# Projecting q and k already turned, and rotating them across partitions with block exchanges by DMA, in a fused attention and FFN kernel

## The chip, the cores and the metric

The kernel runs on one core of one Trainium2 chip. The metric is the device time of one execution in microseconds (us). The kernel before takes 277.16 us, the median of 3 runs (276.86 to 277.42). TensorE is called PE here, VectorE DVE, ScalarE ACT, GpSimd POOL and SyncE SP.

## The reference, cut to what matters

Inputs are x of 8 batches of 1024 tokens by 128, one head of width 128, and an FFN with hidden width 512. Everything is float32. The attention sees `i >= j` only.

```python
def fractional_rope(x, base):                      # first 64 of the 128 features turn, 64 do not
    rot, skip = jnp.split(x, 2, axis=-1)
    even, odd = jnp.split(rot, 2, axis=-1)         # 32 and 32
    return jnp.concatenate([even * cos - odd * sin, even * sin + odd * cos, skip], axis=-1)

q = fractional_rope(x @ wq) / sqrt(128);  k = fractional_rope(x @ wk) / sqrt(128);  v = x @ wv
p = softmax(q @ k.T - 1e30 * (i < j))
x = layernorm(x + (p @ v) @ wo)
h = gelu(x @ (alpha1 * sign(w1)).T + b1)           # exact gelu
x = layernorm(x + h @ (alpha2 * sign(w2)).T + b2)
```

## The kernel before

One batch c (0 to 7) at a time goes through a pipeline of stages, and neighbouring batches overlap. Every engine has a list of calls, written out by hand, which is its program: `scores(3, B - 4)` in PE's list is row tile 3 of batch 4 (B is 8). Engines meet in semaphores alone, and a call that waits holds up all that stands behind it on its engine. This also holds for SP, which issues nearly all DMAs.

A batch has 8 row tiles of 128 tokens, in two halves h. Products that need more than bfloat16 are made of fp32r parts: a value is split into a rounded part (`_hi`) and the rest (`_lo`), and three matmuls (hi by hi, hi by lo, lo by hi) replace one. The stages of a batch:

- SP loads x by stripes (`stripes`), DVE turns it in 32 by 32 squares (`x_squares`), ACT makes `xT_hi`, POOL `xT_lo`.
- `project(h, c)`: 4 token tiles times 3 matmuls of 256 columns each put q and k of half h, tokens on partitions, into a PSUM pair (two banks).
- `rotate(h, c)` on DVE: three products from PSUM with the tables; `rotation_sum` on POOL adds them into `tok`; `tok_copy` on ACT moves the 64 features that do not turn.
- `turn_qk(n, c)`, n from 0 to 3: 4 transposes of 128 by 128 on PE bring q or k of one half into a bank with the features on partitions; `qkT_high` (ACT) and `qkT_low` (DVE) write `qkT_hi` and `qkT_lo`.
- `scores(r, c)` on PE, `row_max` on DVE, `exponentials` on ACT, `turn_row` on DVE (32 by 32 squares); `carry(g, c)` on SP completes the transpose of the probabilities by 16 DMAs for rows 0 to 3 (g = 0), 16 for rows 4 to 7 (g = 1). `weigh_group(g, ..., c)` multiplies by x, `project_out` by wv times wo. Rows 4 to 7 of batches 0 and 7 are turned by PE instead.
- `residual1`, `statistics1` and `first_norm` (DVE), `first_factors` (POOL), `turn_x1`, `up`, `gelu`, `hidden_high` (ACT), `hidden_low` (POOL), `down`, `y_half`, `turn_y`, `residual2`, `statistics2`, `second_factors`, `second_norm` are the first norm, the FFN and the second norm; `store` writes the result.

Three PSUM pairs go round among projections, scores and `up`, and two banks among the rest (`next_pair`, `next_bank`). A call that takes a pair waits until the call three pairs ago has been read. `qkT_hi` and `qkT_lo` exist once: batch c overwrites batch c - 1 there.

Of the kernel before, what the change touches and what calls it, by code (L numbers as in the profile page):

```python
# [5 lines left out]
F32 = mybir.dt.float32  # L6
# [10 lines left out]
def attention_ffn_kernel(nc, x, wq, wk, wv, wo, w1, b1, w2, b2, cos_t, sin_t, out):  # L17
# [12 lines left out]
    P = 128  # L30
# [25 lines left out]
    with ctx:  # L56
# [10 lines left out]
        cos_sb = sb("cos_sb", [P, NT, ROT])  # L67
        sin_sb = sb("sin_sb", [P, NT, ROT])
# [17 lines left out]
        rot_cos = sb("rot_cos", [P, NG, TG, 2, ROT])  # L86
        rot_sin = sb("rot_sin", [P, NG, TG, 2, ROT])
        tok = sb("tok", [P, NT, QK])
# [34 lines left out]
        w2_sb = hid[:, 3, 0:H]  # L123
        w_raw = hid[:, 3, H:H + 2 * D]
# [9 lines left out]
        s_bias_in = sem("s_bias_in")  # L134
        s_xq_in = sem("s_xq_in")
# [68 lines left out]
        def _(sp):  # L204
# [15 lines left out]
            sp.dma_start(b2_sb[:, :], b2.rearrange("(p a) -> p a", a=1)).then_inc(s_bias_in, 16)  # L220

# [36 lines left out]
            stripes(2)  # L258
            carry(0, 0)
            stripes(3)  # L260
            tokens(1)
            stripes(B - 4)
            carry(0, 1)
            carry(1, 1)
            tokens(2)
            stripes(B - 3)
            carry(0, 2)
            carry(1, 2)
            stripes(B - 2)
            tokens(3)  # L270
            carry(0, 3)
            carry(1, 3)
            stripes(B - 1)
            carry(0, B - 4)
            tokens(B - 4)
            tokens(B - 3)
            carry(1, B - 4)
            carry(0, B - 3)
            tokens(B - 2)
            store(0)  # L280
            carry(1, B - 3)
            carry(0, B - 2)
            store(1)
            carry(1, B - 2)
            store(2)
            tokens(B - 1)
            carry(0, B - 1)
            store(3)
            store(B - 4)
            store(B - 3)  # L290
            store(B - 2)
            store_half(0, B - 1)
# [5 lines left out]
        def _(pool):  # L298
# [38 lines left out]
            def xT_low(h, c):  # L337
                pool.wait_ge(s_xT_hi[h], c + 1)
                if c > 0:
                    pool.wait_ge(s_qk[h], c)  # L340
# [3 lines left out]
            def rotation_sum(h, c):  # L344
                pool.wait_ge(s_rot_mul[h], c + 1)
                if c > 0:
                    pool.wait_ge(s_qkT[2 * h + 1], c)
                four = tok[:, TG * h:TG * (h + 1), :].rearrange("p n (j d) -> p n j d", d=D)
                pool.tensor_tensor(four[:, :, :, 0:ROT], rot_cos[:, h, :, :, :], rot_sin[:, h, :, :, :],  # L349
                                   ALU.add).then_inc(s_rot_add[h], 1)  # L350
# [45 lines left out]
            rotation_sum(0, 1)  # L396
            rotation_sum(1, 1)
            xT_low(0, 2)
            xT_low(1, 2)
            rotation_sum(0, 2)  # L400
# [3 lines left out]
            rotation_sum(1, 2)  # L404
            rotation_sum(0, 3)
            first_factors(1, 0)
            xT_low(0, B - 4)
            xT_low(1, B - 4)
            rotation_sum(1, 3)
            first_factors(0, 1)  # L410
            first_factors(1, 1)
            rotation_sum(0, B - 4)
            rotation_sum(1, B - 4)
            hidden_low(0, 0)
            hidden_low(1, 0)
            hidden_low(2, 0)
            xT_low(0, B - 3)
            hidden_low(3, 0)
            first_factors(0, 2)
            xT_low(1, B - 3)  # L420
            first_factors(1, 2)
            rotation_sum(0, B - 3)
            xT_low(0, B - 2)
# [3 lines left out]
            hidden_low(3, 1)  # L427
            first_factors(0, 3)
            second_factors(0)
            rotation_sum(1, B - 3)  # L430
            first_factors(1, 3)
            xT_low(1, B - 2)
            hidden_low(0, 2)
            rotation_sum(0, B - 2)
# [50 lines left out]
        def _(pe):  # L485
# [9 lines left out]
            def wait_freed(task, i, c):  # L495
# [7 lines left out]
                if task == "qk":  # L503
                    pe.wait_ge(s_tok[i], c + 1)
                if task == "up":
                    pe.wait_ge(s_gelu[i], c + 1)
# [1624 lines left out]
```

## Time and profile before

| | |
|---|---|
| time, median of 3 runs | 277.16 us |
| span of the profiled execution, first to last instruction | 274.5 us |
| median time less this span | 2.7 us |
| PE, DVE, ACT, POOL busy | 95%, 84%, 82%, 61% |
| matmul instructions | 1485 |
| bytes moved by DMA | 31.94 MB |

No time of the profiled execution beyond its span is listed; the 2.7 us are the median less the span and stand for what lies around it. The page lists busy time by engine, and the chain that ended last: PE holds 81% of it. SP's time isn't in the busy shares, since issuing a DMA isn't counted as work; it is seen in the timeline alone. Durations of neighbouring instructions on PE and DVE overlap, so that the distance between two starts is what one instruction takes from its engine.

### The profile page before, as it was taken

Reading aid. Unit: us, or ns where it says so; the run is one execution under the profiler, and the core shown is the slowest. Engines: PE = TensorE matmul, PEld = TensorE weight load, DVE = VectorE, ACT = ScalarE, POOL = GpSimd, SP = SyncE. Lnnn points to the kernel's source line nnn. Section 1 sums busy time; section 2 is a strip of 40 time slices with the busy share of each in tenths; the row PEclk is TensorE's granted clock in tenths of the full one; section 3 lists DMA queues with packets and bytes.
Section 4 is the critical chain, followed back from the end, with each engine's and each line's share of the span. In section 5 each row is a group of like instructions: output and inputs, shape, how many; then the busy total and the mean of one; then the engine's idle time right before and its main releaser. Section 6 shows DMA issues by size and latency. Waiting matters only on the chain.

```text
span 274.5 us, 5184 instructions
## 1 busy us (share of the span) xinstructions
PE 260.9 (95%) x1485; PEld 208.7 (76%) x1487; DVE 229.6 (84%) x638; ACT 224.7 (82%) x398; POOL 167.2 (61%) x258
## 2 busy tenths in 40 slices
PE   7899999999999999999999999999999999999960
PEld 3678989987779588868879688868886878897630
DVE  2799999999999996999979987998689738537984
ACT  3378964565897989996998999898999799999972
POOL 3033132613625698399821998497819887887772
PEclk9999999999999999999999999999999999999997
DMA  7944596479657936833685318825830720200323
GB/s 178 166 61 87 107 145 98 115 163 192 104 132 160 199 94 153 180 47 78 173 187 127 82 39 249 184 71 151 189 73 27 197 55 2 76 2 0 111 90 108
DMA packets 58012, 31.94 MB, mean 116 GB/s; under 512 B 33408, under 2 KB 54400, under 8 KB 57984
## 3 DMA queue, kind: packets, MB, share of 16 engines
q1 hardware_dynamic: 57024, 30.76, 50.4%
q10 hardware_dynamic: 960, 0.85, 1.3%
q8 instruction: 12, 0.20, 0.3%
q14 instruction: 16, 0.13, 0.2%
HBM read 9.18 MB, written 4.19 MB: 49 GB/s over the span
## 4 chain that ended last, share of the span: by engine, by line
PE 81%; DVE 6%; ACT 5%; issue 3%; DMA 2%; ACTq 1%; POOL 0%; POOLq 0%
PE pair L589 18%; PE bank L606 18%; PE bank L632 5%; PE bank L674 4%; PE pair L650 4%; PE pair L651 4%; PE bank L620 4%; PE bank L682 4%; PE bank L683 4%; PE bank L719 2%; DMA sin_sb<-in_sin_dram 2%; PE pair L663 2%; PE pair L665 2%; PE pair L664 2%; PE bank L639 2%
## 5 line engine op out<-in xcount | busy, mean ns | idle before, releaser
L391 POOL TENSOR_TENSOR hid_lo<-hid,hid_hi 128x1024 fp32r<-128x1024 f32 x28 | 66.0, 2386 | 19.7 <-ACT hid_hi L1075 19.7
L1004 ACT ACTIVATE prob<-pair,negmax 128x128 f32<-128x128 f32 (+3 forms) x64 | 47.2, 742 | 14.2 <-DVE negmax L1457 12.5
L606 PE MATMUL bank<-probT,xa 128*128 128x512 f32 (+3 forms) x160 | 54.2, 482 | 0.0
L1457 DVE CUSTOM_DVE_ANT_0 pair<-pair,mask_row 128x128 f32<-128x128 f32 (+3 forms) x64 | 47.9, 759 | 6.1 <-PE pair L589 5.5
L606 PEld LDWEIGHTS bank<-probT,xa 128*128 128x128 f32 x160 | 29.1, 190 | 20.2 <-issue 15.3
L341 POOL TENSOR_TENSOR xT_lo<-xT,xT_hi 128x512 fp32r<-128x512 f32 x14 | 18.0, 1288 | 40.4 <-ACT xT_hi L1034 40.4
L1467 DVE STREAM_TRANSPOSE turned<-prob 128x128 f32<-128x128 f32 (+7 forms) x56 | 39.5, 724 | 0.5 <-ACT prob L1004 0.5
L589 PE MATMUL pair<-qkT_hi 128*128 128x512 f32 (+3 forms) x96 | 36.0, 375 | 0.8 <-DVE qkT_lo L1619 0.3
L1068 ACT ACTIVATE hid<-pair,b_sb,alpha 128x1024 f32<-128x1024 f32 x28 | 32.9, 1209 | 0.1
L589 PE MATMUL pair<-qkT_lo,qkT_hi 128*128 128x512 f32 (+3 forms) x96 | 32.8, 342 | 0.0
L589 PE MATMUL pair<-qkT_hi,qkT_lo 128*128 128x512 f32 (+3 forms) x96 | 32.8, 342 | 0.0
L1075 ACT ACTIVATE hid_hi<-hid 128x1024 fp32r<-128x1024 f32 x28 | 28.6, 1057 | 0.0
L335 POOL TENSOR_TENSOR ln<-ln,minus_half 128x4 f32<-128x4 f32 (+1 forms) x21 | 26.2, 1249 | 1.6
L1102 ACT ACTIVATE res<-res,ln 128x128 f32<-128x128 f32 x52 | 23.1, 496 | 3.6 <-POOL ln L377 3.6
L1056 ACT ACTIVATE qkT_hi<-bank 128x512 fp32r<-128x512 f32 x32 | 18.5, 598 | 7.3 <-PE bank L674 7.2
L1619 DVE TENSOR_TENSOR qkT_lo<-bank,qkT_hi 128x512 fp32r<-128x512 f32 x32 | 21.1, 680 | 3.4 <-ACT qkT_hi L1056 3.4
L349 POOL TENSOR_TENSOR tok<-rot_cos,rot_sin 128x512 f32<-128x512 f32 x14 | 18.0, 1288 | 9.4 <-DVE rot_sin L1614 9.4
L650 PE MATMUL pair<-x1T_hi,sgn1T 128*128 128x512 f32 x56 | 23.4, 418 | 0.3 <-issue 0.3
L682 PE MATMUL bank<-hid_hi,sgn2T 128*128 128x512 f32 x56 | 22.3, 399 | 0.0
L683 PE MATMUL bank<-hid_lo,sgn2T 128*128 128x512 f32 x56 | 22.2, 396 | 0.0
L651 PE MATMUL pair<-x1T_lo,sgn1T 128*128 128x512 f32 x56 | 22.1, 395 | 0.0
L1567 DVE TENSOR_TENSOR res<-bank,x 128x512 f32<-128x512 f32 x16 | 10.9, 687 | 12.5 <-PE bank L719 12.4
(116 smaller groups left out, 649.9 us busy)
## 6 DMA issues: line engine op xcount, KB each, us to landing
probT<-turned SPq DMA_DIRECT2D x96, 116.0 KB, 2.3
probT<-turned SPq DMA_DIRECT2D x128, 52.0 KB, 2.0
xq<-in_L_attn_x_dram SPq DMA_DIRECT2D x28, 128.0 KB, 4.0
xa<-in_L_attn_x_dram SPq DMA_DIRECT2D x7, 512.0 KB, 4.7
out_dram<-res SPq DMA_DIRECT2D x7, 512.0 KB, 3.3
hid<-in_L_ffn_w_dram SPq DMA_DIRECT2D x2, 256.0 KB, 3.2
out_dram<-res SPq DMA_DIRECT2D x2, 256.0 KB, 2.3
xa<-in_L_attn_x_dram SPq DMA_DIRECT2D x1, 256.0 KB, 3.6
```

Source lines behind the costliest of these rows:

```text
L391: pool.tensor_tensor(hid_lo[:, j, :], hid[:, j, :], hid_hi[:, j, :].bitcast(F32), ALU.subtract).then_inc(s_hid_lo[j], 1)
L589: ins = pe.matmul(dst[:, lo:hi], qp[:, 0, me], kp[:, 1, lo - first:hi - first], start=n == 0, stop=n == 2)
L606: ins = pe.matmul(bank_of["px", g, c][:, 0:n * P], xa[c % 2][:, j, :], probT[g][:, :, TG * j:TG * j + n, :].rearrange("p n m i -> p m n i" ...
L650: pe.matmul(dst[:, half(h)], sgn1T[:, j, :], x1T_hi[:, half(h)], start=True, stop=False)
L651: ins = pe.matmul(dst[:, half(h)], sgn1T[:, j, :], x1T_lo[:, half(h)], start=False, stop=True)
L682: pe.matmul(dst[:, :], sgn2T[:, j, :], hid_hi[:, j, half(h)], start=j == 0, stop=False)
L683: ins = pe.matmul(dst[:, :], sgn2T[:, j, :], hid_lo[:, j, half(h)], start=False, stop=j == NF - 1)
L1004: act.activation(prob[r % 3][:, 0:(r + 1) * P], pair_of["score", r, c][:, slice(*columns(r))], ACT.Exp, scale=-1.0, bias=negmax[:, r:r + 1 ...
L1068: act.activation(hid[:, j, :], pair_of["up", j, c][:, :], ACT.Gelu, bias=b1_sb[:, j:j + 1], scale=alpha1[:, j:j + 1]).then_inc(s_gelu[j], 1)
L1075: act.activation(hid_hi[:, j, :], hid[:, j, :], ACT.Copy).then_inc(s_hid_hi[j], 1)
L1457: dve.tensor_tensor_reduce(mine, mine, mask_row[:, T - (r + 1) * P:T], -1.0, -MASKED, ALU.add, ALU.min, negmax[:, r:r + 1]).then_inc(s_max ...
L1467: dve.transpose(turned[g][:, :, squares(r, 0, r), :].rearrange("p k m j -> p m k j"), prob[r % 3][:, 0:(r + 1) * P].rearrange("p (m k j) - ...
```

## The change

Batch 0 is computed as before. From batch 1 on, q and k are projected with the weights as the stationary operand and x as the moving one, so the result has the features on partitions at once. The weight columns are reordered: `project_rot` gives the 64 turning features of q and the 64 of k, `project_skip` the 64 others of each; each is 6 matmuls of 512 columns. The rotation then needs the partner 32 features away, that is 32 partitions away. ACT copies the turning part into `rotT`, SP exchanges its four blocks of 32 partitions into `swapT` (`swap`, 4 DMAs), DVE multiplies `rotT` by the cosines (`rot_cos_part`), POOL `swapT` by the sines (`rot_sin_part`), DVE adds (`rot_sum`) and rounds into `rotT` (`rot_high`), POOL makes the rest in `swapT` (`rot_low`), and SP moves both into the first 64 partitions of `qkT_hi` and `qkT_lo` (`moves`, 2 and 2 DMAs). The other 64 partitions are written from PSUM by `skip_high` (ACT) and `skip_low` (DVE). `project`, `rotate`, `tok_copy`, `turn_qk`, `qkT_high`, `qkT_low` remain for batch 0 only, and their buffers share memory with later ones. Two transposed tables are loaded as well.

```diff
@@ SP @@
+            def swap(c):
+                sp.wait_ge(s_tok[0], c + 1)
+                if c > 1:
+                    sp.wait_ge(s_rot_in, 16 * 4 * (c - 1))
+                for n in range(NB):
+                    m = n ^ 1
+                    sp.dma_start(swapT[n * BLK:(n + 1) * BLK, :].bitcast(F32), rotT[m * BLK:(m + 1) * BLK, :].bitcast(F32)).then_inc(s_swap_in, 16)
+            def moves(c):
+                sp.wait_ge(s_score[NT - 1], c)
+                sp.wait_ge(s_rot_add[1], c + 1)
+                for j in range(2):
+                    sp.dma_start(qkT_hi[0:ROT, j, :].bitcast(F32), rotT[j * ROT:(j + 1) * ROT, :].bitcast(F32)).then_inc(s_rot_in, 16)
+                sp.wait_ge(s_rot_pool, 2 * c)
+                for j in range(2):
+                    sp.dma_start(qkT_lo[0:ROT, j, :].bitcast(F32), swapT[j * ROT:(j + 1) * ROT, :].bitcast(F32)).then_inc(s_rot_in, 16)
...
@@ POOL @@
-            def rotation_sum(h, c):
-                pool.wait_ge(s_rot_mul[h], c + 1)
...
+            def rot_sin_part(c):
+                pool.wait_ge(s_swap_in, 16 * NB * c)
+                pool.tensor_tensor(swapT[:, :].bitcast(F32), swapT[:, :].bitcast(F32), sinT[:, :], ALU.mult).then_inc(s_rot_pool, 1)
+            def rot_low(c):
+                pool.wait_ge(s_rot_add[1], c + 1)
+                pool.tensor_tensor(swapT[:, :], turnT[:, :], rotT[:, :].bitcast(F32), ALU.subtract).then_inc(s_rot_pool, 1)
@@ PE @@
             def scores(r, c):
-                for n in (0, 1) if r < TG else (2, 3):
-                    pe.wait_ge(s_qkT_lo[n], c + 1)
+                elif r == 0:
+                    pe.wait_ge(s_rot_in, 16 * 4 * c)
+                    pe.wait_ge(s_qkT_lo[0], c + 1)
+                    pe.wait_ge(s_qkT_lo[1], c + 1)
...
+            def project_turned(dst, w, c):
+                pe.wait_ge(s_xT_lo[0], c + 1)
+                pe.wait_ge(s_xT_lo[1], c + 1)
+                cols = slice(w * D, (w + 1) * D)
+                for h in range(NG):
+                    pe.matmul(dst[:, half(h)], w_lo[:, cols], xT_hi[:, half(h)], start=True, stop=False)
...
@@ ACT @@
+            def rot_copy(c):
+                act.wait_ge(s_qk[0], c + 1)
+                act.activation(rotT[:, :].bitcast(F32), pair_of["rot", 0, c][:, :], ACT.Copy).then_inc(s_tok[0], 1)
+            def skip_high(j, c):
+                act.wait_ge(s_qk[1], c + 1)
+                act.wait_ge(s_score[NT - 1], c)
+                act.activation(qkT_hi[ROT:D, j, :], pair_of["skip", 0, c][j * ROT:(j + 1) * ROT, :], ACT.Copy).then_inc(s_qkT_hi[j], 1)
...
@@ DVE @@
+            def rot_cos_part(c):
+                dve.wait_ge(s_tok[0], c + 1)
+                dve.tensor_tensor(turnT[:, :], rotT[:, :].bitcast(F32), cosT[:, :], ALU.mult).then_inc(s_rot_mul[0], 1)
+            def rot_sum(c):
+                dve.wait_ge(s_rot_pool, 2 * c - 1)
+                dve.tensor_tensor(turnT[:, :], turnT[:, :], swapT[:, :].bitcast(F32), ALU.add).then_inc(s_rot_add[0], 1)
+            def rot_high(c):
+                dve.tensor_copy(rotT[:, :], turnT[:, :]).then_inc(s_rot_add[1], 1)
+            def skip_low(j, c):
+                dve.tensor_tensor(qkT_lo[ROT:D, j, :], pair_of["skip", 0, c][j * ROT:(j + 1) * ROT, :], qkT_hi[ROT:D, j, :].bitcast(F32), ALU.subtract).then_inc(s_qkT_lo[j], 1)
```

The lists of calls of all engines are new. Three places matter below. The first is the start of PE's program, after the first two transposes of q and k of batch 0. `warm` matmuls only keep PE busy; `hid` holds wv there. Before:

```order
L674 MATMUL bank<-ident,tok 128x128 x8
L489 MATMUL pair<-warm 128x512 x6
L551 MATMUL bank<-ident,hid 128x128
L589 MATMUL pair<-qkT_hi 128x128
L589 MATMUL pair<-qkT_lo,qkT_hi 128x128
```

And of the change:

```order
L755 MATMUL bank<-ident,res_0 128x128 x8
L541 MATMUL pair<-warm 128x512 x6
L736 MATMUL pair<-xT_hi,w_lo 128x512 x2
L738 MATMUL pair<-xT_hi,w_hi 128x512 x2
L740 MATMUL pair<-xT_lo,w_hi 128x512 x2
L755 MATMUL bank<-ident,res_1 128x128 x4
L651 MATMUL pair<-qkT_hi 128x128
```

The projection `project_rot(1)` and the turn of q's second half now stand ahead of `scores(0, 0)`, the row in `qkT_hi` of 128x128.

The second place is SP's program around the carries of batch 3 (before also the first of batch 4). `probT<-turned` are the carries (32x416 rows 0 to 3, 32x928 rows 4 to 7), `xq` the stripes, `xa` the token load. Before:

```order
L242 DMA probT<-turned 32x416 x16
L242 DMA probT<-turned 32x928 x16
L226 DMA xq<-in_L_attn_x_dram 32x32x32 x4
L242 DMA probT<-turned 32x416 x16
L231 DMA xa<-in_L_attn_x_dram 128x8x128 x2
```

And of the change:

```order
L251 DMA swapT<-rotT 32x1024 x4
L272 DMA probT<-turned 32x416 x16
L258 DMA qkT_hi<-rotT 64x1024 x2
L261 DMA qkT_lo<-swapT 64x1024 x2
L242 DMA xa<-in_L_attn_x_dram 128x8x128
L272 DMA probT<-turned 32x928 x16
L237 DMA xq<-in_L_attn_x_dram 32x32x32 x4
```

Each batch now has 8 more issues in this queue, and the four of `moves` stand ahead of the second carry.

The third is DVE's program around the last rows' maxima (`negmax<-pair`) of batch 4 before, batch 5 after, where the next batch's rotation stands. Before:

```order
L1490 BN_STATS stat<-res 128x6 [waits s_res15]
L1611 TENSOR_TENSOR rot_cos<-pair,cos_sb 128x512 [waits s_rot_add0,s_qk0]
L1612 TENSOR_TENSOR rot_sin<-pair,sin_sb 128x8x32
L1614 TENSOR_TENSOR rot_sin<-pair,sin_sb 128x8x32
L1619 TENSOR_TENSOR qkT_lo<-bank,qkT_hi 128x512 [waits s_qkT_hi0]
L1619 TENSOR_TENSOR qkT_lo<-bank,qkT_hi 128x512 [waits s_qkT_hi1]
```

And of the change:

```order
L1668 TENSOR_TENSOR turnT<-rotT,cosT 128x1024 [waits s_rot_pool,s_tok0]
L1606 TENSOR_TENSOR x1T_lo<-bank,x1T_hi 128x512 [waits s_x1T_hi0]
L1606 TENSOR_TENSOR x1T_lo<-bank,x1T_hi 128x512 [waits s_x1T_hi1]
L1503 ISA pair,negmax<-pair,mask_row 128x896 [waits s_score6]
```

Where DVE read PSUM and one table, it now reads two SBUF tensors of 1024 columns, and twice a batch: here, and in the sum.

## Rows read from the trace of the kernel before

**Rows 1.** The page, parts 1 and 2: busy time by engine, then in 40 slices.
```profile
PE 260.9 (95%) x1485; PEld 208.7 (76%) x1487; DVE 229.6 (84%) x638; ACT 224.7 (82%) x398; POOL 167.2 (61%) x258
```
**Rows 2.** Busy time by engine in four stretches.
```profile
0.00:40.00 40.00, 36.90 (x229) 29.00 (x231) 32.84 (x77) 26.46 (x63) 11.65 (x20) 1.00 0.68 122
40.00:212.20 172.20, 171.73 (x965) 137.82 (x964) 157.06 (x428) 146.43 (x252) 109.11 (x164) 1.00 0.58 131
...
225.10:274.50 49.40, 39.37 (x227) 30.98 (x226) 33.08 (x117) 41.05 (x69) 35.37 (x49) 0.96 0.17 54
```
**Rows 3.** The chain that ended last, 27 to 42 us: start, length, what.
```profile
27.42 0.44 PE bank L674 x4
...
32.56 0.74 PE pair L589 x6
33.30 0.12 PE pair L663
...
35.26 2.16 PE bank L606 x8
37.41 2.63 PE pair L589 x15
```
**Rows 4.** PE's timeline, start and duration: two matmuls of 512 columns.
```profile
132.18 0.39 PE L651 MATMUL pair<-x1T_lo,sgn1T 128*128 128x512 f32 x1
132.41 0.39 PE L650 MATMUL pair<-x1T_hi,sgn1T 128*128 128x512 f32 x1
```
**Rows 5.** Instructions by line and form: busy, mean ns, idle before.
```profile
L1619 DVE TENSOR_TENSOR qkT_lo<-bank,qkT_hi 128x512 fp32r<-128x512 f32 x32 | 21.1, 680 | 3.4 <-ACT qkT_hi L1056 3.4
L1611 DVE TENSOR_TENSOR rot_cos<-pair,cos_sb 128x512 f32<-128x512 f32 x16 | 10.9, 679 | 1.7 <-DMA sin_sb<-in_sin_dram 1.4 <-PE pair L665 0.2
L1457 DVE CUSTOM_DVE_ANT_0 pair<-pair,mask_row 128x1024 f32<-128x1024 f32 x8 | 9.9, 1235 | 0.3 <-PE pair L589 0.2
L1612 DVE TENSOR_TENSOR rot_sin<-pair,sin_sb 128x256 f32<-128x256 f32 x16 | 6.6, 414 | 0.0
L1444 DVE TENSOR_TENSOR w_lo<-hid,w_hi 128x256 fp32r<-128x256 f32 x1 | 0.4, 426 | 0.0
L1442 DVE CAST w_hi<-hid 128x256 fp32r<-128x256 f32 x1 | 0.3, 294 | 1.5 <-DMA hid<-in_L_attn_wk_dram 1.5
L1056 ACT ACTIVATE qkT_hi<-bank 128x512 fp32r<-128x512 f32 x32 | 18.5, 598 | 7.3 <-PE bank L674 7.2
L1075 ACT ACTIVATE hid_hi<-hid 128x1024 fp32r<-128x1024 f32 x28 | 28.6, 1057 | 0.0
L391 POOL TENSOR_TENSOR hid_lo<-hid,hid_hi 128x1024 fp32r<-128x1024 f32 x28 | 66.0, 2386 | 19.7 <-ACT hid_hi L1075 19.7
L349 POOL TENSOR_TENSOR tok<-rot_cos,rot_sin 128x512 f32<-128x512 f32 x14 | 18.0, 1288 | 9.4 <-DVE rot_sin L1614 9.4
```
**Rows 6.** DVE's timeline at the start.
```profile
10.26 0.69 DVE L1589 TENSOR_TENSOR tok<-rot_cos,rot_sin 128x512 f32<-128x512 f32 x1
13.93 1.78 DVE L1589 TENSOR_TENSOR tok<-rot_cos,rot_sin 128x512 f32<-128x512 f32 x1
```
**Rows 7.** POOL's timeline at the same place.
```profile
13.87 1.29 POOL L341 TENSOR_TENSOR xT_lo<-xT,xT_hi 128x512 fp32r<-128x512 f32 x1 [10.23 <-ACT xT_hi L1034]
```
**Rows 8.** SP's timeline: start, time of all issues of the row.
```profile
20.18 10.84 SPq L242 DMA_DIRECT2D probT<-turned  x16
...
122.91 10.02 SPq L242 DMA_DIRECT2D probT<-turned  x16
...
212.29 10.84 SPq L242 DMA_DIRECT2D probT<-turned  x16
```
**Rows 9.** What SP's queue waited for, 40 to 190 us: total, times, longest.
```profile
SPq L242 <- DVE turned L1467: 12.5, 5, 6.2
```
**Rows 10.** DVE's timeline before the last first-half carry.
```profile
211.51 0.70 DVE L1467 STREAM_TRANSPOSE turned<-prob 128x512 f32<-128x512 f32 x1
```
**Rows 11.** The page, part 6: DMAs, KB each, us from issue to landing.
```profile
probT<-turned SPq DMA_DIRECT2D x128, 52.0 KB, 2.0
```

More of the change, by code:

```diff
@@ L850, in _ @@
-            turn_qk(0, B - 3)
-            turn_qk(1, B - 3)
+            project_skip(B - 3)
+            weigh_group(1, 0, 3, 3)
+            weigh_group(1, 4, 7, 3)
+            down(0, 1)
+            down(1, 1)
             up(0, 2)
             up(1, 2)
-            down(0, 1)
-            down(1, 1)
+            turn_y(0, 1)
+            project_out(1, 3)
             up(2, 2)
-            turn_y(0, 1)
+            turn_y(1, 1)
+            project_rot(B - 2)
             up(3, 2)
-            turn_y(1, 1)
@@ L886, in _ @@
-            turn_qk(3, B - 2)
-            project(0, B - 1)
-            down(1, 2)
-            turn_y(0, 2)
+            project_rot(B - 1)
+            weigh_group(0, 0, 3, B - 3)
+            turn_x1(0, B - 4)
             scores(0, B - 2)
@@ L1734, in _ @@
             first_norm(7, 0)
-            statistics1(0, 1)
-            turn_row(4, 2)
-            row_max(7, 2)
-            x1T_low(1, 0)
-            turn_row(5, 2)
-            turn_row(6, 2)
-            reciprocals(0, 2)
+            residual1(0, 1)
+            residual1(1, 1)
+            residual1(2, 1)
+            residual1(3, 1)
+            x1T_low(0, 0)
+            turn_row(4, 2)
+            x_squares(0, B - 4)
+            row_max(6, 2)
+            x_squares(1, B - 4)
+            row_max(7, 2)
+            rot_sum(3)
+            x1T_low(1, 0)
+            skip_low(0, 3)
+            skip_low(1, 3)
+            rot_high(3)
+            statistics1(0, 1)
             statistics1(1, 1)
@@ L1846, in _ @@
-            statistics1(3, 3)
-            turn_row(4, B - 4)
-            x1T_low(0, 2)
             row_max(7, B - 4)
             x1T_low(1, 2)
+            skip_low(0, B - 3)
+            skip_low(1, B - 3)
+            x_squares(0, B - 2)
+            x_squares(1, B - 2)
+            rot_sum(B - 3)
+            rot_high(B - 3)
+            reciprocals(0, B - 4)
+            turn_row(6, B - 4)
+            residual2(0, 1)
             residual1(4, 3)
+            statistics1(1, 3)
+            statistics1(2, 3)
@@ L2105, in rotation_tables @@
         rows = np.concatenate(halves, axis=1).reshape(T // P, P, 2 * half)
-        tables.append(np.ascontiguousarray(rows.transpose(1, 0, 2)))
+        by_tokens = rows.transpose(1, 0, 2).reshape(P, T // P * 2 * half)
+        turned = np.concatenate(halves * 2, axis=1).T
+        tables.append(np.ascontiguousarray(np.concatenate((by_tokens, turned), axis=1)))
     return tables
```

1110 lines of the change are left out of this document (544 added, 566 removed).

## The prediction

> **What bounds the kernel now.** I read busy time first [rows 1]: PE has 95% of the span and most of the chain. The stretches [rows 2] say where: from 40.0 to 212.2 us PE is busy 171.7 of 172.2 us and has no gap worth naming, so here the kernel takes what PE's instructions take. But the others are near: DVE is busy 157.1 of 172.2 (91%), ACT 146.4, POOL 109.1. SP shows in no busy share. Its timeline [rows 8] shows that one carry of 16 DMAs takes 10.02 us when nothing holds it, 0.626 us an issue. A batch has two carries (but batches 0 and 7), 4 stripes, a token load and a store, 38 issues or some 24 us of the 29.8 us that lie between two batches (212.29 less 122.91, over 3 [rows 8]), and in 150 us of the middle SP waited only 12.5 us for DVE's turned rows [rows 9]. So I ask of each engine how early it could reach one milestone: M, the start of the last first-half carry, 212.3 us now. DVE ends the turn of row 3 of the last batch at 212.2 us [rows 8, 10], so DVE's work leads to it. From M the kernel needs 12.8 us to the first weighing of batch 7 (10.84 issues and 2.0 landing [rows 8, 11]) and 49.4 us to the end [rows 2].
>
> **PE.** The 16 transposes of a batch go. Four take 0.44 us [rows 3]; 28 groups in batches 1 to 7 make 12.3 us. The projection does not change: 24 matmuls of 256 columns at 0.12 us [rows 3] were 2.9 us, 12 of 512 at 0.23 us (132.41 less 132.18 [rows 4]) are 2.8. I add 1 us for restarts after transposes, an estimate between 0 and 2. These waits and reads of `tok` on ACT and POOL go too, but were hidden.
>
> **The start pays back part of it.** `project_rot(1)` (2.8 us) now stands before `scores(0, 0)`, with its wait for both halves of `xT_lo`, about 0.7 us more. The turn of row 3, which released the first carry at 20.2 us [rows 8], and two squares of x that DVE now does earlier put that carry at about 24.3. It takes 10.8 us; `moves(1)` stands behind it, so it begins at 35.1, its four issues take 2.5, and they land 2.0 later [rows 11]: 39.6, say 40. Only then may `scores(0, 1)` start, which ran at 32.6 [rows 3]. From 32.56 to 40.04 PE was never idle; of these 7.5 us only a projection of 12 times 0.12 us can still run before 40, so 6.1 us of scores and weighing [rows 3] are now late; the projections done by then are the same. PE alone: 40 + 234.5 (the rest of the span) + 6.1 - 10.6 (24 groups after 40 us) - 1 = 269.0 us of span. PE's own gain is 5.5.
>
> **DVE.** Removed in a batch, two `rotate` of 679 + 414 + 414 ns and four `qkT_low` of 680 [rows 5]: 5.73 us. Added: two sums or products of 1024 columns and two `skip_low`, also of 1024 though on 64 partitions. No row shows them; the nearest is the row maximum of 1024 columns, 1235 ns [rows 5], and two products of 512 would be 1.36 us. `rot_high` is a rounding: 256 columns took 294 ns where a difference took 426 [rows 5], so it goes at two columns a cycle; from that 0.69 us, at worst 1.24. Sum 5.6 (5.6 to 6.7), so -0.1 to +1.0 a batch; I take +0.2, 1.5 us over seven.
>
> The lock comes on top. The same DVE sum of two SBUF tensors took 0.69 us at 10.26 and 1.78 us at 13.93 [rows 6]. POOL's difference ran from 13.87 to 15.16 [rows 7]: 15.16 + 0.6 is where DVE's ended. It waited for POOL. The Trainium skill says the same in "SBUF — State Buffer", section Who interferes with whom: a DVE instruction with two SBUF inputs and a POOL instruction that reads SBUF block each other for a whole instruction; by this rule, the trace agrees, both new sums are exposed, and so is a two-port rounding, which no row here shows blocked. POOL is busy 109.1 of 172.2 us, and more after: its two sums of 1288 ns become two of 2386 [rows 5], 2.2 us a batch or 15 us. It stays below DVE's load. With POOL busy two times in three and instructions up to 2.4 us long, a meeting costs 0.8 us on average. Of the product each batch I count five meetings (POOL has little to do for batches 1 and 2), 4 us, and 1 us for the sum, which mostly follows POOL's own product while POOL waits for DVE. Total 5; the ends are 0 and 14 times 2.4, 33.
>
> DVE to M: 32.8 + 157.1 = 189.9 us busy [rows 2], +1.5, +5, and -2.3 for the residuals, statistics and norms of batches 3 and 6 that now stand behind the turn (some 12 short instructions less two `x1T_low`, an estimate). DVE idled 7.2 us in the first 40 and 4 more fall to the start above: 11. Sum 205.1, if it never waits again. It waited 15.1 us between 40 and 212, because PE was late; with PE relieved I leave 1.4. M = 206.5.
>
> **ACT.** Six copies of 598 ns become three of 1057 (three instructions of 1024 columns [rows 5]), 3.6 to 3.2 us; nothing, and it is less loaded before M.
>
> **SP.** 8 more issues a batch. No row has 32 or 64 partitions of 4 KB; the nearest is the carry, 0.626 us, so 5.0 us a batch. After `moves(1)` at 37.6, before M stand 12 carries (120 us), 48 exchanges and moves (30), 16 stripes (10), 7 token loads and 2 stores (5): M is not before 202.6. A batch costs SP 29 us. That leaves 4 us for all its waits if M is to be 206.5.
>
> The Trainium skill, in "DMA: Bandwidth & Descriptors", section Issuing engines are not separate DMA queues, calls the sequencer's time to start a DMA usually small beside the DMA itself. By that rule the 56 issues would cost nothing; 0.626 of a landing time of 2.0 us [rows 8, 11], 56 times, is 35 us, and the row decides.
>
> **The sum.** The latest of the three is DVE's, M = 206.5. Behind it 12.8 + 49.4, and 2 us because rows 6 and 7 of batch 7 (2.6 us of PE) now stand behind the weighing while some turning moved ahead: 270.7 us. PE's own sum, 269.0, and SP's, 266.8, are below. The median of the runs is 2.7 us over the span: 273.4 us, 1.4% less than 277.16. The likeliest case reaches from 270 (no lock, PE's sum) to 276.5.
>
> **Rivals.**
> - The gain of PE arrives nearly whole. The start's loss is made up because scores of batch 1 were not urgent and DVE's late work moves into the last 49.4 us, where DVE is idle 16.3 [rows 2]: 277.2 - 12.3 - 1 = 264, with half the start's loss 267. Against it: DVE's 91%. Chance 0.14.
> - SP decides, and it is slower. `moves(c)` waits for the last score of c - 1, for DVE's rounding and POOL's rest, and the second carry of c - 1 stands behind it; `swap` waits for ACT's copy. Before, SP's waits were 12.5 us [rows 9] while it had 6 us a batch to spare; now it has almost none. M is 202.6 plus the waits, the time M + 66.9. It is slower than before from 8.2 us of waits on. With 2.5 us a batch, 15 in all, 284.5. For it: three engines in a row must be on time. Against it: a queue that is late finds its waits over. Chance 0.2.
> - The lock decides: POOL has a full 2.4 us instruction ahead of most of the 14 sums, 20 us in all where I took 5. M = 221.5, but late work of DVE can be put off by some 8: about 280. Slower from 4.3 us beyond my 5. Chance 0.12.
> - Nothing changes: three engines within a few us of each other hand waits round, and M stays where DVE's 15 us of idle time have it. 277. Chance 0.1.
>
> **How the numbers follow.** The forecast has 0.44. Range: 266.5 to 282 us; what is left out is the tail of the whole gain and of the SP case. A change under 0.2% (0.55 us) can't be told from none. Faster: 0.44 and 0.14 and a little of "nothing changes", 0.6; same 0.08; slower 0.32.
>
> **What the new profile would show.** PE: 112 transposes fewer and gaps, its busy share down to some 92%. A wait of PE of 3 us or more before the first score tile of batch 1 at about 40 us. DVE over 94% from 40 us to M, its two new sums above 1.24 us on average (by 0.4 us) and longest where POOL runs. SP with no idle time but short ones, an issue of the new kinds at 0.6 us. M at 206 to 207. I am wrong if the first score tile of batch 1 runs before 36 us, if the new DVE sums show no lengthening, if SP's issues of 4 KB rows take 0.4 us or below, or if M moves by less than 2 us.

## The result

The changed kernel takes 327.85 us (median of 4 runs, 325.71 to 329.02) against 277.01 us for the kernel before (275.94 to 277.42). The ratio is 1.183, with a 95% interval of 1.177 to 1.189. The forecast of 273.4 us was wrong by 54 us and in the sign, and the range up to 282 does not hold it. Where an execution in the experiments below lies more than 1.5% above the fastest of its run, the ratio leaves it out, and a second median, in brackets, is the one without it and is used for differences.

The busy line of the page after, against [rows 1]:

```profile
PE 270.8 (83%) x1291; PEld 204.6 (63%) x1291; DVE 264.2 (81%) x603; ACT 226.3 (70%) x377; POOL 188.9 (58%) x258
```

No engine is over 83%. PE has 194 instructions fewer (1485 to 1291) and is busy 10 us longer; DVE has 35 fewer and is busy 35 us longer. So something makes instructions longer, and something makes engines wait. The stretches are cut at 40 us, at the start of batch 6's first-half carry, and where the issues of the last first-half carry end (columns: stretch, its length, busy time of each engine, mean granted clock of TensorE, DMA share, GB/s):

```profile
0.00:40.00 40.00, 29.51 (x162) 21.23 (x162) 29.75 (x56) 22.54 (x48) 12.53 (x19) 1.00 0.82 168
40.00:213.27 173.27, 151.54 (x694) 114.90 (x694) 153.13 (x339) 120.72 (x198) 107.52 (x141) 0.92 0.74 162
213.27:254.00 40.73, 38.86 (x174) 28.24 (x174) 31.10 (x78) 36.35 (x58) 27.83 (x33) 0.96 0.57 143
254.00:325.30 71.30, 50.91 (x265) 40.24 (x263) 50.17 (x132) 46.72 (x75) 41.03 (x65) 0.91 0.15 46
```

In a middle of nearly the same length (173.3 against 172.2 us) PE does 694 matmuls where it did 965, is idle for 22 us where it was never idle, and had 0.92 of its clock where it had all. At 213 us the kernel is one batch behind. From the end of those issues the kernel takes 71.3 us, against 51.4 before (274.5 less 223.1 [rows 8]).

VectorE's first norms, which the change does not touch, before (busy and mean ns of one; then idle time before them):

```profile
L1499 DVE TENSOR_SCALAR x<-res,ln 128x128 f32<-128x128 f32 x64 | 18.7, 340 | 0.6 <-POOL ln L369 0.3
```

And after, with the four kinds of operation that the change adds to VectorE:

```profile
L1545 DVE TENSOR_SCALAR x<-res,ln 128x128 f32<-128x128 f32 x64 | 44.1, 737 | 4.1 <-POOL ln L379 3.0 <-POOL ln L421 1.1
L1684 DVE TENSOR_TENSOR qkT_lo<-pair,qkT_hi 64x1024 fp32r<-64x1024 f32 x14 | 17.1, 1223 | 1.3 <-ACT qkT_hi L1110 1.0
L1668 DVE TENSOR_TENSOR turnT<-rotT,cosT 128x1024 f32<-128x1024 f32 x7 | 12.3, 1761 | 0.0
L1674 DVE TENSOR_TENSOR turnT<-turnT,swapT 128x1024 f32<-128x1024 f32 x7 | 8.5, 1215 | 0.6 <-POOL swapT L396 0.6
L1679 DVE CAST rotT<-turnT 128x1024 fp32r<-128x1024 f32 x7 | 5.8, 831 | 0.2
```

The norms alone have 25.4 of VectorE's 34.6 us more. The timeline shows where they get it (start, length, what). VectorE at seven of batch 4's eight first norms, which stand ahead of batch 6's row maxima:

```profile
197.17 1.07 DVE L1545 TENSOR_SCALAR x<-res,ln 128x128 f32<-128x128 f32 x4
199.73 4.94 DVE L1545 TENSOR_SCALAR x<-res,ln 128x128 f32<-128x128 f32 x3 [1.49 <-POOL ln L379]
204.59 0.28 DVE L1503 CUSTOM_DVE_ANT_0 pair<-pair,mask_row 128x128 f32<-128x128 f32 x1
```

POOL beside it, and TensorE behind it:

```profile
199.66 4.67 POOL L443 TENSOR_TENSOR hid_lo<-hid,hid_hi 128x1024 fp32r<-128x1024 f32 x2
```

```profile
202.10 0.34 PE L651 MATMUL pair<-qkT_hi,qkT_lo 128*128 128x384 f32 x1
206.84 0.79 PE L651 MATMUL pair<-qkT_hi 128*128 128x512 f32 x1 [4.40 <-ACT prob L1057]
207.43 0.63 PE L651 MATMUL pair<-qkT_lo,qkT_hi 128*128 128x512 f32 x1
210.16 0.39 PE L651 MATMUL pair<-qkT_lo,qkT_hi 128*128 128x512 f32 x1
```

Four norms took 1.07 us ahead of POOL's two subtractions; three took 4.94 us beside them, and end 0.3 us after POOL. (The prediction calls this the lock; below it is POOL's hold.) The row maximum of row 0 of batch 6 stands behind the norms on VectorE, ScalarE's exponentials behind that, and the next score tile needs their buffer: PE waits 4.40 us. Of this, 1.28 us are a load of ScalarE's function table, which starts only when VectorE is done (205.03 us). PE comes back slow: the matmul of 512 columns at 207.43 took 0.63 us, the one at 210.16 took 0.39. The page's row of granted clock, in tenths by slices of 8.1 us, has a 5 there (the 26th slice), the 1.2 GHz level, and further dips; [rows 2] had none in the middle:

```profile
PEclk9999979959799899999999799599899996998998
```

The dips follow waits (of 2.71 us before 42.9, 3.17 before 66.9, 3.97 before 291.8, for example), so a wait costs more than its length.

Waits by releaser (us in total, times, longest; PE's matmuls and its weight loads, PEld, are listed apart, though they are the same waits), and landing times (count, KB, median us from issue to landing), against [rows 11]:

```profile
POOL swapT L396 <- DMA swapT<-rotT: 29.2, 5, 10.7
DVE pair L1503 <- PE pair L651: 17.9, 21, 4.4
PEld bank L701 <- DVE x L1545: 16.4, 7, 6.8
PEld pair L651 <- DMA qkT_lo<-swapT: 11.1, 5, 3.6
```

```profile
probT<-turned SPq DMA_DIRECT2D x96, 116.0 KB, 3.0
probT<-turned SPq DMA_DIRECT2D x128, 52.0 KB, 1.9
swapT<-rotT SPq DMA_DIRECT2D x28, 128.0 KB, 3.2
qkT_hi<-rotT SPq DMA_DIRECT2D x14, 256.0 KB, 3.5
qkT_lo<-swapT SPq DMA_DIRECT2D x14, 256.0 KB, 4.4
```

PE waits more for VectorE's norms than for the moves. The moves hold a second engine: `rot_copy` of the next batch overwrites `rotT` and so waits until they have landed (a wait that the excerpt of the change doesn't show), 15.0 us in all. The new transfers land in 3.2 to 4.4 us where I took 2.0, and the large carries need 3.0 where they needed 2.3. The start of the last first-half carry, the milestone M, lies in this row, which holds two carries:

```profile
231.17 22.91 SPq L272 DMA_DIRECT2D probT<-turned  x32
```

The first carry's 16 issues end at 241.8 us, SyncE waits for VectorE's turned row, and the last one's start at 244.07. M is 244.1 us against 212.3 [rows 8].

### The profile page after: what moved, and what is told of

It is laid out like the page before. It is cut to its first block, busy times and chain, and to the rows that moved or that the text cites. A ratio compares the mean times of both kernels' runs of the same rounds, so it can differ in the third digit from the quotient of the medians.

```text
span 325.3 us, 4732 instructions
## 1 busy us (share of the span) xinstructions
PE 270.8 (83%) x1291; PEld 204.6 (63%) x1291; DVE 264.2 (81%) x603; ACT 226.3 (70%) x377; POOL 188.9 (58%) x258
## 3 DMA queue, kind: packets, MB, share of 16 engines
q1 hardware_dynamic: 60896, 42.82, 58.3%
## 4 chain that ended last, share of the span: by engine, by line
PE 24%; DVE 17%; POOL 16%; SPq 15%; issue 14%; DMA 11%; ACT 2%; POOLq 0%; ACTq 0%; DVEq 0%
SPq L272 9%; PE pair L651 8%; DMA qkT_lo<-swapT 6%; PE bank L668 6%; POOL hid_lo L443 5%; DVE x L1545 5%; DVE turned L1513 3%; DMA xq<-in_L_attn_x_dram 3%; SPq L237 3%; POOL ln L379 2%; POOL swapT L402 2%; PE bank L694 2%; DMA swapT<-rotT 2%; DVE pair L1503 1%; POOL swapT L396 1%
## 5 line engine op out<-in xcount | busy, mean ns | idle before, releaser
L668 PE MATMUL bank<-probT,xa 128*128 128x512 f32 (+3 forms) x160 | 59.4, 524 | 0.4 <-DMA probT<-turned 0.4
L651 PE MATMUL pair<-qkT_hi 128*128 128x512 f32 (+3 forms) x96 | 38.6, 402 | 17.5 <-DMA qkT_lo<-swapT 9.6
L668 PEld LDWEIGHTS bank<-probT,xa 128*128 128x128 f32 x160 | 32.8, 209 | 27.6 <-issue 22.1
L1545 DVE TENSOR_SCALAR x<-res,ln 128x128 f32<-128x128 f32 x64 | 44.1, 737 | 4.1 <-POOL ln L379 3.0
L651 PE MATMUL pair<-qkT_lo,qkT_hi 128*128 128x512 f32 (+3 forms) x96 | 35.7, 372 | 0.0
L651 PEld LDWEIGHTS pair<-qkT_hi 128*128 128x128 f32 x96 | 20.4, 213 | 22.6 <-DMA qkT_lo<-swapT 11.1
L396 POOL TENSOR_TENSOR swapT<-swapT,sinT 128x1024 f32<-128x1024 f32 x7 | 17.5, 2502 | 29.2 <-DMA swapT<-rotT 29.2
L1531 DVE SCALAR_TENSOR_TENSOR res<-bank,rinv,xa 128x128 f32<-128x128 f32 x64 | 19.0, 340 | 14.2 <-issue 8.9
L402 POOL TENSOR_TENSOR swapT<-turnT,rotT 128x1024 fp32r<-128x1024 f32 x7 | 16.7, 2390 | 20.9 <-DVE rotT L1679 20.9
L701 PE MATMUL bank<-ident,x 128*128 128x128 f32 x64 | 12.1, 324 | 16.3 <-DVE x L1545 13.7
```

Source lines behind the costliest of these rows:

```text
L402: pool.tensor_tensor(swapT[:, :], turnT[:, :], rotT[:, :].bitcast(F32), ALU.subtract).then_inc(s_rot_pool, 1)
L651: ins = pe.matmul(dst[:, lo:hi], qp[:, 0, me], kp[:, 1, lo - first:hi - first], start=n == 0, stop=n == 2)
L668: ins = pe.matmul(bank_of["px", g, c][:, 0:n * P], xa[c % 2][:, j, :], probT[g][:, :, TG * j:TG * j + n, :].rearrange("p n m i -> p m n i" ...
L1545: ins = dve.tensor_scalar(x1[c % 2][:, t, :], res1[:, t, :], ln1[:, 2, t:t + 1], ln1[:, 7, t:t + 1], ALU.subtract, ALU.mult)
```

## The experiments

Times are medians, ratios are to the kernel before on the same chip (276.7 to 277.2 us), with 95% intervals. Where one kernel is compared with the changed one, its 327.85 us is of another group of runs.

### Is it the exchange as a chain, SyncE's queue, or POOL's hold on VectorE?

**b_issues**: the kernel before, with eight issues more a batch on SyncE.

```diff
+            def spare_four(n):
+                sp.wait_ge(s_spare_in, 16 + 64 * n)
+                for j in range(NB):
+                    part = slice(j * BLK, (j + 1) * BLK)
+                    sp.dma_start(spare[part, :], spare[part, :]).then_inc(s_spare_in, 16)
             carry(0, 0)
+            spare_four(0)
...
+            spare_four(1)
             carry(0, 1)
```

> The kernel before with 8 more DMA issues a batch in SP's queue (batches 1 to 7), four behind each first-half carry and four ahead of the next, each copying 32 partitions of 2 KB onto themselves; nobody waits for them. The sine table is left out (the cosines stand in), which makes room. Theory chain (the exchange makes scores late, SP's issues alone are harmless): within 3 us of before, 277 to 280. Rival SP (the queue itself was full, as the forecast feared): 285 or more, with weighings waiting for carries.

Measured: 296.54 us (295.1), 1.070 (1.063 to 1.077). Copies that nobody but the queue waits for cost 19 us. Its queue from 107 us on:

```profile
107.12 11.15 SPq L244 DMA_DIRECT2D probT<-turned  x16
118.31 2.49 SPq L251 DMA_DIRECT2D spare<-spare  x4
120.90 10.11 SPq L244 DMA_DIRECT2D probT<-turned  x16
131.11 2.85 SPq L228 DMA_DIRECT2D xq<-in_L_attn_x_dram  x4
134.00 3.79 SPq L251 DMA_DIRECT2D spare<-spare  x4
```

One issue takes 0.62 us, and here the queue has no gap in which a late carry could catch up; the last first-half carry starts at 232.29 us. The late carries reach PE, which waited 0.3 us for them before:

```profile
PEld bank L629 <- DMA probT<-turned: 7.6, 4, 3.8
```

**a_free**: the changed kernel, whose scores no longer wait for the moves. The second pair of moves copies `swapT` onto itself. It leaves out the rotated half of q and k in the scores of batches 1 to 7, which use batch 0's, and the sine table.

```diff
-                    sp.dma_start(qkT_hi[0:ROT, j, :].bitcast(F32), rotT[j * ROT:(j + 1) * ROT, :].bitcast(F32))
+                    sp.dma_start(aside[j * ROT:(j + 1) * ROT, :].bitcast(F32), rotT[j * ROT:(j + 1) * ROT, :].bitcast(F32))
...
-                    pe.wait_ge(s_rot_in, 16 * 4 * c)
```

> The changed kernel with the same DMA issues, but the two moves go to a tile of their own and back onto the source, so that the scores of batches 1 to 7 do not wait for them (they use batch 0's turned half, one table stands in for the other). Theory chain: PE's 20.7 us of waits for the landing of moves go, and with them the low clock that follows and part of the lock's 25 us, so 328 falls to 300 or below. Rival lock (the norm and rounding instructions of DVE that POOL blocks are the cause by themselves): 315 to 325. Rival order (the new lists are worse whatever the exchange does): 315 or more.

Measured: 325.99 us, 1.180 (1.174 to 1.186). PE's own wait for the moves is not what costs. It was 11.1 us and not the 20.7 expected, which added PE's and PEld's account of the same waits. With it gone, PE waits more for the norms, and ScalarE's copy still waits for the landing:

```profile
PEld bank L704 <- DVE x L1548: 19.9, 9, 6.7
ACT rotT L1107 <- DMA swapT<-swapT: 11.0, 4, 5.8
```

**b_nohid and a_nohid**: both kernels, with the hidden layer's low halves computed in batch 0 only.

```diff
-                pool.tensor_tensor(hid_lo[:, j, :], hid[:, j, :], hid_hi[:, j, :].bitcast(F32),
-                                   ALU.subtract).then_inc(s_hid_lo[j], 1)
+                if c == 0:
+                    pool.tensor_tensor(hid_lo[:, j, :], ...).then_inc(s_hid_lo[j], 1)
+                else:
+                    pool.wait_ge(s_hid_lo[j], c)
+                    pool.memset(idle_cell[:, j:j + 1], 0.0).then_inc(s_hid_lo[j], 1)
```

> Control: the kernel before with POOL's difference hid_lo of 2.4 us computed for batch 0 only; later calls write one column of four instead. No DVE norm waited for POOL before, and PE was full, so every theory expects 274 to 278; only the last batch's end may be shorter.

> The changed kernel with the same cut: hid_lo computed for batch 0 only. POOL then has nothing of 2.4 us to block DVE with but the two rotation sums. Theory lock: the 25 us that the first norm's instructions lost go, and with them PE's idle time behind them: 300 or below. Theory chain: the waits of scores for moves stay, 310 to 320.

Measured: 276.73 us for b_nohid, 1.000 (0.997 to 1.002), and 308.23 us for a_nohid, 1.113 (1.105 to 1.121). The same 24 subtractions (4 of the 28 are batch 0's and stay) cost nothing in the order of before and 19.6 us in the new one. The norms in a_nohid, which still meet POOL's sine product:

```profile
L1550 DVE TENSOR_SCALAR x<-res,ln 128x128 f32<-128x128 f32 x64 | 22.7, 402 | 3.3 <-POOL ln L380 2.2 <-POOL ln L422 1.1
```

**a_split**: was it the hold, or is POOL merely sooner free for the rotation? Nothing is left out here; each subtraction is cut in four.

```diff
+                for q in range(4):
+                    cols = slice(q * T // 4, (q + 1) * T // 4)
+                    ins = pool.tensor_tensor(hid_lo[:, j, cols], hid[:, j, cols], hid_hi[:, j, cols].bitcast(F32),
+                                             ALU.subtract)
+                ins.then_inc(s_hid_lo[j], 1)
```

> The changed kernel with each low half of the hidden layer taken on POOL in four pieces of 256 columns instead of one of 1024: nothing is left out, POOL has the same elements and a little more to start. In the changed kernel single first norms of VectorE last up to 2.5 us beside one such subtraction (2.4 us), 44 us in all against 19 before. Theory of the hold (a norm that writes SBUF from SBUF gets in only between two instructions of POOL): with pieces of some 0.65 us no norm waits for more than one piece, the norms fall to 23 to 30 us busy and the time to 308 to 318. Rival (what a_nohid gained comes from POOL being free sooner for the rotation's work, not from VectorE): POOL is no sooner free here, so 325 to 330.

Measured: 312.0 us, 1.127 (1.119 to 1.134). POOL is busy 12 us longer (201.0) and the kernel 16 us shorter. The norms:

```profile
L1548 DVE TENSOR_SCALAR x<-res,ln 128x128 f32<-128x128 f32 x64 | 25.6, 448 | 3.1 <-POOL ln L379 2.0 <-POOL ln L421 1.1
```

The longest norm fell from 2.52 us (2.42 beside a subtraction) to 0.89, where a piece of a subtraction takes 0.76. So the hold is shown: a norm gets in between two POOL instructions, and their length is the price. This is the best complete version of the change, and still 35 us behind.

### The exchange and the hold together

**a_nodma and a_nodma_nohid**: no swap and no move at all, with and without the hidden layer's subtractions.

```diff
-            swap(1)
-            moves(1)
...
-                pool.wait_ge(s_swap_in, 16 * NB * c)
-                pool.tensor_tensor(swapT[:, :].bitcast(F32), swapT[:, :].bitcast(F32), sinT[:, :],
+                pool.wait_ge(s_tok[0], c + 1)
+                pool.tensor_tensor(swapT[:, :].bitcast(F32), rotT[:, :].bitcast(F32), sinT[:, :],
...
-                    pe.wait_ge(s_rot_in, 16 * 4 * c)
+                    pe.wait_ge(s_rot_pool, 2 * c)
```

> The changed kernel without any swap or move (the sine part reads rotT where it stands, the scores of the later batches use the first batch's rotated half, which is what is left out), and with POOL's work on the hidden layer kept. It is the fourth corner beside the changed kernel (327.9), a_nohid (308.2) and a_nodma_nohid (292.3). If the two causes add up, the exchange costs the same 16 us with the hold as without it: 309 to 315. If they share their cost (a late SyncE is what pushes the norms beside POOL's subtractions), taking away the exchange alone gives nearly all: 292 to 300. If the hold hides the exchange: 322 or more.

> The changed kernel without any swap or move, and with the low halves of the hidden layer in the first batch only: every operation of the five engines stays (the sine part reads rotT where it stands, and the scores of the later batches use the first batch's rotated half, which is what is left out), but 56 issues and 11 MB are gone. It gives what the new orders and the 28 transposes fewer come to when no exchange is paid for. Theory: the exchange is the loss, and the rest gives TensorE's 12 us back: 264 to 272. Rival: the new orders themselves lose, whatever the exchange: 280 or more.

Measured: 323.2 us, 1.166 (1.160 to 1.171), and 292.3 us; of the latter's four executions two took 289.8 and 290.4 us, the others 294.2 and 294.4, so 290.1 is used, without an interval. With the hold the exchange costs 4.7 us, without it 18.1; with the exchange the hold costs 19.6 us, without it 33.1. So the hold hides most of the exchange, as the third guess for a_nodma had it. In a_nodma_nohid the rival's side came true: with no exchange and without those subtractions the new kernel is still 13 us slower than before. Its middle:

```profile
100.00:160.00 60.00, 58.48 (x269) 42.98 (x269) 58.85 (x145) 51.58 (x82) 37.27 (x73) 1.00 0.55 120
```

VectorE is at 98% there, and PE at 97. **a_norot_nohid** takes the rotation's work away, here on VectorE and likewise POOL's two operations.

```diff
-                dve.tensor_tensor(turnT[:, :], rotT[:, :].bitcast(F32), cosT[:, :], ALU.mult)
+                dve.tensor_tensor(turnT[:, 0:1], rotT[:, 0:1].bitcast(F32), cosT[:, 0:1], ALU.mult)
...
-                dve.tensor_copy(rotT[:, :], turnT[:, :])
+                dve.tensor_copy(rotT[:, 0:1], turnT[:, 0:1])
```

> a_nodma_nohid (292.3) with the rotation's five operations of a batch (cosine part, sum and rounding on VectorE, sine part and low half on POOL) cut to one column each: what is left out is the rotation from the second batch on. VectorE loses 26 us of the 241 in which it was busy, POOL 33. In a_nodma_nohid VectorE is busy 98% of the stretch from 100 to 160 us. Theory (VectorE's load is what keeps that run above the kernel before): 270 to 278. Rival (the order of work, with its longer start, is the reason, and VectorE is busy because it is behind): 286 to 292.

Measured: 283.3 us (282.9), 1.024 (1.019 to 1.030), between the two guesses. The rotation's work, 22 us on VectorE and 34 on POOL, is worth 7 us; which engine's share counts was not tried apart. The last 6 us stay without any rotation, exchange or hold:

```profile
PE 253.2 (91%) x1291; PEld 193.9 (70%) x1291; DVE 219.3 (79%) x603; ACT 224.2 (81%) x377; POOL 98.3 (35%) x258
```

PE has 7.7 us less to do than before and the kernel is 6 us longer; of PE's busy time in the first 40 us 7.0 are missing (29.9 against 36.9). That is the late start, and the order behind it; which of them has how much was not tried.

### What of the exchange costs: issues, bytes or waits?

**b_act_issues**: the spare issues of b_issues from ScalarE's queue. **a_act and a_act_nohid**: the same with the changed kernel's swaps and moves.

```diff
@@ in ScalarE's program @@
             rot_copy(2)
+            swap(2)
...
+            moves(2)
             xT_high(1, 3)
             pxT_copy(1, 0)
             rot_copy(3)
```

> The kernel before with the same 56 spare issues as in the run b_issues (four at a time, 64 KB each, cosines standing in for the sines), but issued from ScalarE's queue, not SyncE's: four ahead of the first exponential of a batch and four ahead of its seventh. The bytes and the DMA engines' work are those of b_issues. Theory: what costs in b_issues is SyncE's queue, which is never idle and so starts every later carry later; then most of its 20 us go away and the time is 277 to 284 (ScalarE pays for the issues, but it waits 50 us in the kernel before). Rival: the DMA engines' traffic, or the waits inside, is what costs; then it stays at 292 to 300. If an issue holds ScalarE for 0.6 us as it does SyncE, ScalarE has 34 us more to do, and 284 to 292 would be this price and not the traffic's.

> The changed kernel with the swaps and the moves issued from ScalarE's queue: a swap right behind the copy of q and k into rotT, the moves three or so operations ahead of the next such copy. SyncE has only what it had in the kernel before. Theory (SyncE's queue costs about 20 of the 50 us, and POOL's hold on VectorE 20 more): 300 to 312. Rival (the queue's cost is not additive, since the transfers' latency or the traffic is what the batches wait for): 320 to 328.

> The same as a_act, and with the low halves of the hidden layer computed in the first batch only (the part of the computation that is left out), so that POOL has no long subtractions beside VectorE's first norms, as in a_nohid (308 us). Theory of two nearly additive causes: 282 to 292. Rival (one cause seen twice, so that taking away the second gives little): 300 to 308.

Measured: b_act_issues 289.2 us, 1.043 (1.038 to 1.049), inside the range that was expected for ScalarE's own price; a_act 341.9 us, 1.235 (1.227 to 1.242); a_act_nohid 326.7 us, 1.177 (1.170 to 1.184). For the changed kernel both guesses fall, in both runs: it is 14 and 18 us slower than from SyncE. The rows of a_act say why. An issue holds ScalarE as long as SyncE, and ScalarE has work of its own queued behind:

```profile
126.98 1.15 ACTq L1085 DMA_DIRECT2D qkT_hi<-rotT  x2
128.18 2.21 ACTq L1088 DMA_DIRECT2D qkT_lo<-swapT  x2
130.49 3.40 ACT L1118 ACTIVATE hid<-pair,b_sb,alpha 128x1024 f32<-128x1024 f32 x3 [2.36 <-issue]
```

In these runs the queue's cost and ScalarE's delay can't be told apart.

**b_issues_small, a_free_nohid and a_small_nohid**: the issues stay, the bytes go.

```diff
-                    sp.dma_start(spare[part, :], spare[part, :])
+                    sp.dma_start(spare[part, 0:16], spare[part, 0:16])
```

a_free_nohid is a_free and a_nohid in one; a_small_nohid cuts its swaps and moves to `0:16` in the same way, and its sine part reads `rotT`.

> The kernel before with the 56 spare issues on SyncE's queue as in b_issues (296.5), but each moves 16 columns of its 32 partitions (2 KB) and not 64 KB. Issues, their places in the queue and their waits are the same, the bytes are nearly gone. Theory (the time that an issue holds SyncE's queue costs): 290 to 298. Rival (the traffic of 3.7 MB costs, beside the carries): 277 to 282.

> a_free and a_nohid in one: the moves go aside, so that no score waits for them (the scores of the later batches use the first batch's rotated half, and one table stands for both, which is left out), and the hidden layer's low halves are taken in the first batch only. All 56 issues and all bytes stay. In a_nohid (308.2) TensorE still waits 21 us for the moves. Theory (what costs beside the hold is SyncE's queue and not the latency of the moves): 303 to 309. Rival (behind the hold the moves' latency was hidden, and it decides once the hold is gone): 292 to 300, near the 292.3 of the run without any exchange.

> a_free_nohid (306.8) with 16 columns in every swap and move and not 1024 (the sine part reads rotT where it stands once the swap has landed; the scores of the later batches use the first batch's rotated half, and the hidden layer's low halves are taken in the first batch only: these are left out). 56 issues stay in their places, 11 MB go. Theory (the issues' time in SyncE's queue costs): 302 to 308. Rival (bytes and landing times cost): 290 to 296, near the 292.3 of the run without any exchange.

Measured: b_issues_small 296.7 us (296.4), 1.071 (1.065 to 1.077); a_free_nohid 306.8 us (305.0; a fourth execution took 509.6 us, and its cause is open), 1.104 (1.096 to 1.112); a_small_nohid 293.8 us (293.2), 1.058 (1.049 to 1.068). In the kernel before 64 KB or 2 KB an issue makes no difference: the queue's time costs all 19 us. In the changed kernel it is the reverse: 56 issues almost without bytes cost 3 us (293.2 against 290.1, in which single executions differ by as much), the bytes 12 (305.0 against 293.2). I had expected the issues in both. The landing times of a_free_nohid:

```profile
probT<-turned SPq DMA_DIRECT2D x96, 116.0 KB, 2.8
swapT<-rotT SPq DMA_DIRECT2D x28, 128.0 KB, 3.1
swapT<-swapT SPq DMA_DIRECT2D x14, 256.0 KB, 4.4
```

And of a_small_nohid:

```profile
probT<-turned SPq DMA_DIRECT2D x96, 116.0 KB, 2.3
swapT<-rotT SPq DMA_DIRECT2D x28, 2.0 KB, 1.9
swapT<-swapT SPq DMA_DIRECT2D x14, 4.0 KB, 1.8
```

Taking the bytes away shortens both the landing of the exchange and that of the carries beside it. It also ends ScalarE's wait for the landing before its next copy into `rotT`, which a_small_nohid doesn't have and a_free_nohid does:

```profile
ACT rotT L1112 <- DMA swapT<-swapT: 13.3, 5, 6.0
```

PE waits 7.7 us for that copy in a_free_nohid and 0.8 in a_small_nohid. A second `rotT` would test it; how the 12 us divide among the three is open.

## Why the prediction was wrong

The loss, taken away in one order (others divide it otherwise, since the causes overlap, and executions of one kernel differ by up to 5 us): 327.9, less 19.6 for the hidden layer's subtractions, whose cost is the hold on the norms, less 15.0 for the exchange's bytes and waits, less 3.1 for its issues, less 7.2 for the rotation's work on VectorE and POOL, less 5.9 for the start and the order, is the kernel before, 277.0.

In the terms of the prediction's sum for VectorE: up to M it was busy 210.4 us where the sum had 194.1, and idle 33.6 us where it left 12.4. Of the 16 us more of work, 12.7 are the first norms (27.0 us against 14.3 before).

- **PE's term was right in kind.** 112 transposes went, and where the clock stays up (a_norot_nohid, 0.988 against 0.993) PE is busy 253.2 us against 260.9, 7.7 us less where the sum had 12.3. But it needed a kernel that PE bounds, and the new one is not. In it PE is busy longer than before, because its clock falls to 1.2 GHz after waits; the sum had no term for that.
- **The start was nearly right.** The first score tile of batch 1 was forecast at 40 us, after a wait of 3 us or more:

```profile
42.90 0.48 PE L651 MATMUL pair<-qkT_hi 128*128 128x128 f32 x1 [2.71 <-DMA qkT_lo<-swapT]
```

  PE's busy time up to 40 us fell by 7.4 us where I counted 6.1 later work. The 2.9 us between 40 and 42.9 are mostly the landing time taken too short.
- **The lock was mis-sized, and on the wrong instructions; this is the step that failed most.** I wrote "Total 5" for the product and the sum of the rotation. The product did lengthen, to 1.76 us on average and 3.45 at most, 3.8 us in all, as counted; the sum did not (1.22), and the rounding did once (1.67 us). But the 64 first norms were in neither the sum nor its bounds, since in the profile before no norm was longer than 0.44 us. There only two of them started while POOL was in a long instruction, and within 0.4 us of its end (at 125.03 and 225.90 us); b_nohid shows that the subtractions cost nothing then. The lists of calls of all engines are new, and that broke it: 25.4 us on VectorE, 20 to 33 us of time. Not all of it is the hidden layer's subtractions: at 79.08 us a norm took 2.52 us beside the new sine product on POOL, and the norms of a_nohid keep 4.0 us of the 25.4. The rival "the lock decides" (0.12; 280) had the mechanism, but for the 14 rotation instructions only. The rule that I cited from the Trainium skill ("SBUF — State Buffer", Who interferes with whom) goes on to name tensor-scalar operations among those that can take the shared pair of ports; the norms are such, and these rows agree. I had read it for the added instructions alone.
- **VectorE's net work** came out near: added 17.1 + 12.3 + 8.5 + 5.8 = 43.7 us for seven batches, of which 4 is the hold, removed 40.1. But a_norot_nohid shows that the rotation's work, VectorE's and POOL's, costs 7 us all the same, where I let M follow from a sum of busy times with 1.4 us left for waits.
- **SyncE's term failed as a bound.** An issue was 0.59 to 0.63 us, as taken. "That leaves 4 us for all its waits" treated the queue as free to run up to its sum. From 40 us to M SyncE issued for some 176 of 204 us and waited 24, as the others were late for it. M moved by 32 us the other way, to 244.1. The rival "SP decides" (0.2; 284.5) had the direction and, for the kernel before, a cost; in the changed kernel the issues themselves are worth 3 us. SyncE's waits before, which the rival puts at 12.5 us, were those for turned rows up to 190 us alone; with a token load and a store they are 28.4 from 40 to 212. What the slack of 6 us a batch missed is that a queue of 16-issue carries in which each waits for one engine and is waited for by another does not absorb delays: b_issues, where the queue waited 1.8 us for rows in all, has 35 us of issues more against 42 us of such slack, and lost 19 us.
- **Landing times** were taken from the 52 KB carry, 2.0 us. They are 3.2, 3.5 and 4.4. ScalarE's wait for them, 15.0 us, was in no term.
- **The tail** was read as a constant, 12.8 + 49.4 + 2 = 64.2 us from M to the end of the span. It took 81.2 (244.1 to 325.3): it holds norms, subtractions and late work of the batch before too, and its 16 norms took 17.1 us where they took 4.4.
- **The tests named** came out so: PE's share is 83% and not 92; VectorE is at 89% from 40 us to M (180.7 of 204.1) and not over 94; the issues take 0.6 us, as said; the sum is not lengthened and the product is; M moved by far more than 2 us, but back.

The second rule I weighed, that the sequencer's time to start a DMA is usually small (the Trainium skill, "DMA: Bandwidth & Descriptors", Issuing engines are not separate DMA queues), gets both answers here: 56 issues cost 19 us in the kernel before (b_issues_small) and 3 us in the changed one (a_small_nohid).

## What to carry to other kernels

When a change reorders programs, list what never overlapped before and would cost if it did, the short VectorE instructions from SBUF to SBUF beside long POOL instructions first; a profile without such a meeting gives them no price, so bound them by count times POOL's longest instruction, and keep POOL's instructions short. Three resources near their limit are not three bounds of which the latest decides: give each hand-over between them a wait, and let the range go to the side of slower by the sum of the mechanisms, not by each alone. Before moving work from a bound engine to DMA, try its price in the kernel as it is, with spare issues and with no bytes; this prices that kernel alone, 19 us here against 3 in the changed one.

## What had not been expected of the hardware

- An issue costs its engine 0.6 us at either size tried: 2.49 us for four of 64 KB and 2.50 for four of 2 KB on SyncE, 2.47 for four on ScalarE.
- A norm of 128 columns, a tensor-scalar operation from SBUF to SBUF, was 0.34 us at the median, and up to 2.52 us beside POOL's sine product and 2.42 beside a POOL subtraction, both of 1024 columns. Cutting the subtractions in four brought the mean from 737 to 448 ns.
- The exchange lengthens transfers that are not part of it: the 116 KB carries landed in 2.3 us where the packets of the queue took 50.4% of 16 engines' span (before), in 3.0 us at 58.3% (after), and in 2.3 us again in the changed kernel without the exchange (a_nodma). The 3.7 MB of b_issues did not do it (2.3 us).
